# Weight dequantisation one step later, two of its pieces and twelve residual sums beside the feed-forward's first group

## The reference

```python
def nf4_quant_dequant(w):                       # blocks of 64
    absmax = jnp.max(jnp.abs(flat), axis=1, keepdims=True)
    normalized = flat / jnp.where(absmax == 0, 1.0, absmax)
    bounds = (NF4_CODE[:-1] + NF4_CODE[1:]) * 0.5
    idx = jnp.searchsorted(bounds, normalized)
    return (NF4_CODE[idx] * absmax).reshape(shape)
...
q, k, v = h @ Wq, h @ Wk, h @ Wv                # 32 query heads, 8 key-value heads of 128
gs = jax.nn.log_sigmoid(k) / GATE_NORM
o_lin = gla_scan(softmax(q), softmax(k), v, gs) # gated linear attention
y = sliding_window_attn(rope(q), rope(k), v)    # window of 64
o = (0.5 * y + 0.5 * o_lin).astype(bfloat16) @ Wo
...
h = jax.nn.silu(x @ dq1.T) * (x @ dq2.T)        # 512 -> 1376 -> 512
return h @ dq3.T
...
x = x + _layernorm(attention(_layernorm(x)))
x = x + _layernorm(feed_forward(_layernorm(x)))
```

## Time and profile before

| | us |
|---|---|
| median of three runs | 1944.27 |
| the profiled execution | 1944.25 |
| its span, first to last instruction | 1942.5 |
| TensorE busy | 1859.2 (96%) |
| VectorE busy | 1486.0 (77%) |
| ScalarE busy | 1236.8 (64%) |
| GpSimd busy | 1264.9 (65%) |
| mean granted TensorE clock | 0.993 of full speed |
| TensorE waiting for `kt` L945, 29 times | 29.2 |
| TensorE waiting for `xn` at the start, once | 11.5 |
| TensorE waiting for `qtT` L955, 11 times | 9.2 |
| TensorE waiting for `qc` L520, 3 times | 8.6 |

### The profile page before, as it was taken

The page is one execution under the profiler, slowest core; times in us unless marked ns, Lnnn a source line. Parts: engine busy times, 40 slices in busy tenths (PEclk is TensorE's granted clock), DMA queues, the critical chain, the costliest instruction groups (busy, mean ns, idle before and its releaser), DMA issues.

```text
span 1942.5 us, 42961 instructions
## 1 busy us (share of the span) xinstructions
PE 1859.2 (96%) x11566; PEld 1235.4 (64%) x11566; DVE 1486.0 (77%) x3980; ACT 1236.8 (64%) x4840; POOL 1264.9 (65%) x1164
## 2 busy tenths in 40 slices
PE   4899999999999999999999999999999999999997
PEld 3667666766666666766766666766766654444443
DVE  5998888888888888888888888888899956302122
ACT  5677777777777777777777777777667645412121
POOL 2777777777777777777777777777767747212121
PEclk8999999999999999999999999999999999999999
DMA  6111111111111111111111111111201024000000
GB/s 220 55 36 43 41 45 43 43 44 44 43 43 43 42 42 42 43 47 42 42 42 42 42 42 42 42 42 42 84 30 30 23 71 147 33 0 22 0 22 22
DMA packets 85452, 90.52 MB, mean 47 GB/s; under 512 B 14216, under 2 KB 56456, under 8 KB 85384
## 3 DMA queue, kind: packets, MB, share of 16 engines
q1 hardware_dynamic: 85384, 89.71, 14.8%
HBM read 76.48 MB, written 13.18 MB: 46 GB/s over the span
## 4 chain that ended last, share of the span: by engine, by line
PE 62%; DVE 18%; issue 14%; POOL 4%; ACT 1%; DVEq 1%; DMA 0%; POOLq 0%; ACTq 0%
PE bank L1363 17%; PE bank L1352 8%; PE bank L1391 6%; PE bank L1334 4%; PE bank L1407 4%; PE bank L1428 4%; PE bank L1489 4%; PE bank L1400 3%; DVE f_s L1055 2%; PE bank L1318 2%; DVE f_nrm L1042 2%; PE bank L1417 2%; POOL hl L600 2%; PE bank L1507 2%; PE bank L1410 2%
## 5 line engine op out<-in xcount | busy, mean ns | idle before, releaser
L554 POOL TENSOR_TENSOR f_acc<-f_acc,f_s 128x512 f32<-128x512 f32 x429 | 547.5, 1276 | 32.6 <-POOL f_acc L554 0.4
L1363 PE MATMUL bank<-wh,xh 128*128 (+2 forms) x1024 | 334.9, 327 | 6.6 <-DVE cumh L1204 6.0
L1363 PE MATMUL bank<-wl,xh 128*128 (+2 forms) x1024 | 334.8, 327 | 0.0
L1363 PE MATMUL bank<-wh,xl 128*128 (+2 forms) x1024 | 334.6, 327 | 0.0
L538 POOL TENSOR_TENSOR pr<-pr,rp 128x512 f32<-128x512 f32 x128 | 133.2, 1041 | 241.8 <-DVE rp L977 241.5
L1055 DVE TENSOR_SCALAR f_s<-f_nrm 128x512 f32<-128x512 f32 x480 | 260.9, 603 | 3.5
L651 ACT ACTIVATE qe<-bank,nqm 128x128 f32<-128x128 f32 x512 | 180.9, 365 | 108.6 <-DVE qs L906 78.1
L1489 PE MATMUL bank<-xh,w 128*128 (+3 forms) x704 | 218.3, 379 | 1.4 <-ACT sg L832 1.4
L600 POOL TENSOR_TENSOR hl<-hf,hh 128x512 f16<-128x512 f32 (+1 forms) x44 | 51.3, 1167 | 231.9 <-ACT hh L838 231.9
L679 ACT ACTIVATE pr<-bank,pmx 128x128 f32<-128x128 f32 x512 | 180.8, 367 | 32.4 <-DVE pmx L970 24.3
L1214 DVE SCALAR_TENSOR_TENSOR hf<-bank,sg 128x512 f32<-128x512 f32 (+1 forms) x44 | 30.3, 689 | 220.5 <-PE bank L1489 205.9
(11 more groups left out here) (178 smaller groups left out, 4975.0 us busy)
## 6 DMA issues: line engine op xcount, KB each, us to landing
f_blk<-wa SPq DMA_DIRECT2D x33, 320.0 KB, 2.9
f_raw<-wb SPq DMA_DIRECT2D x33, 256.0 KB, 2.7
dequantised<-f_w SPq DMA_DIRECT2D x33, 256.0 KB, 2.0
w<-dequantised SPq DMA_DIRECT2D x33, 256.0 KB, 4.3
raw_qkv<-wq SPq DMA_DIRECT2D x29, 256.0 KB, 2.4
raw_o<-wo SPq DMA_DIRECT2D x29, 256.0 KB, 2.6
f_recb<-scales SPq DMA_DIRECT2D x99, 64.0 KB, 2.6
f_absb<-scales SPq DMA_DIRECT2D x99, 64.0 KB, 2.6
```

The source lines that it names most:

```text
L554: nc.gpsimd.tensor_tensor(f_acc[:], f_acc[:], f_s[:, step, :], ALU.add).then_inc(s["f_ad"], 1)
L1363: last = nc.tensor.matmul(dst, av, w[:, sl + c, lo:hi], start=(n == 0), stop=(n == 3 * NC - 1))
```

## The change

Step 0 makes no comparisons; steps 1 to 31 make pieces 0 to 30, in the turns of the pattern 2, 4, 5, 4. Pieces 31 and 32 are both made beside group 0: 4, 5, 2, 2, 2 comparisons of piece 31 in chunks 1 to 5 and three times 5 of piece 32 in chunks 6 to 8, in the same ring of four slots. The blocks' maxima found in step i are those of piece i, no longer of piece i + 1, and those of piece 32 stand in chunk 2. The low half of a piece (`nf4_low`) goes from the head of turn p = 2 to turn p = 3, after the decays' `gl` and ahead of the comparisons. The twelve residual sums of group 0 go from GpSimd (c = 3 to 5) to VectorE (c = 4 to 6, just ahead of the new rows' statistics). The low halves of a transposed tile are split two ahead and two behind `hidden`. SyncE's tail is put in another order.

```diff
-NF4_STEPS_FIRST = (range(0, 0), range(0, 2), range(2, 8), range(8, 15))
+NF4_FIRST = 1
+NF4_IN_TURNS = STEPS - NF4_FIRST
 NF4_STEPS = (range(0, 2), range(2, 6), range(6, 11), range(11, 15))
...
-        LATE_STEPS = {5: range(0, 3), 6: range(3, 7), 7: range(7, 11), 8: range(11, 15)}
+        LATE_STEPS = {1: (31, range(0, 4)), 2: (31, range(4, 9)), 3: (31, range(9, 11)), 4: (31, range(11, 13)),
+                      5: (31, range(13, 15)), 6: (32, range(0, 5)), 7: (32, range(5, 10)), 8: (32, range(10, 15))}
+        late_number = lambda j, k: 15 * (j - NF4_IN_TURNS) + k
+        late_slot = lambda j, k: late_number(j, k) % 4
...
             with sp.Fori(1, 5) as k:
                 for c in range(NC):
                     load_weights(c, k + 1, k * NC + (NC + c))
-                    nf4_transfers(k * NC + c, 0, 0)
+                    nf4_transfers(k * NC + (c - NF4_FIRST), 0, 0)
...
-            sp.wait_ge(s["f_out"], 16 * 31)
+            sp.wait_ge(s["f_out"], 16 * 30)
...
-            store_piece(31)
-            load_maxima(32, 2)
+            store_piece(30)
+            load_maxima(31, 2)
...
+            store_rows(32)
+            load_piece(32)
+            load_reciprocals(32, 2)
...
-            sp.wait_ge(s["f_ad"], 14 * STEPS)
-            sp.wait_ge(s["f_out"], 16 * STEPS)
-            load_w12(8)
-            load_w12(9)
-            load_w3(9)
             sp.wait_ge(r["x1"], TILES - 2)
             load_w12(10)
+            load_maxima(32, 2)
+            store_piece(31)
+            sp.wait_ge(s["f_out"], 16 * 32)
+            load_w3(9)
             store_piece(32)
             sp.wait_ge(s["f_out"], 16 * NF4_PIECES)
             load_w3(10)
...
-                        if 3 <= c <= 5:
-                            for t in range((c - 2) * STEP, (c - 1) * STEP):
-                                residual(t)
                         if c in LATE_STEPS:
-                            late_add(LATE_STEPS[c])
+                            late_add(*LATE_STEPS[c])
...
+            def residual(t):
+                dve.wait_ge(xr_in[t % (2 * STEP)], 16 * (t // (2 * STEP) + 1))
+                dve.wait_ge(r["z"], t + 1)
+                nc.vector.tensor_tensor(rows[:, t, :], rows[:, t, :], xr[t % (2 * STEP)][:], ALU.add).then_inc(r["x1"], 1)
...
             def turn(t):
-                if t.p == 1 and not (isinstance(t.i, int) and t.i == 0):
-                    nf4_end(t.i - 1)
-                if t.p == 2 and not (isinstance(t.i, int) and t.i == 0):
-                    nf4_low(t.i - 1)
+                if t.p == 1 and not (isinstance(t.i, int) and t.i <= NF4_FIRST):
+                    nf4_end(t.i - (NF4_FIRST + 1))
...
                 log_decay(t)
                 low_decay(t)
-                if t.p > first:
+                if t.p == 3 and not (isinstance(t.i, int) and t.i <= NF4_FIRST):
+                    nf4_low(t.i - (NF4_FIRST + 1))
+                if t.p:
                     nf4(t)
...
-                if t.p == 2 * first:
-                    nf4_blocks(t.i + 1)
-                    nf4_rows(t.i + 1)
+                if t.p == (2 if isinstance(t.i, int) and t.i == 0 else 0):
+                    nf4_blocks(t.i)
+                    nf4_rows(t.i)
...
-            nf4_low(31)
+            nf4_low(30)
             statistics("att", later(1))
+            nf4_scaled(31)
+            late_nf4(*LATE_STEPS[1])
             for c in range(2, FC):
                 if c == TURN_FROM:
                     later_shift("new")
                 if c == FC - 1:
                     nf4_low(32)
-                for item in within[c]:
+                for item in within[c][0:2]:
                     low(item)
                 hidden(0, c)
+                for item in within[c][2:]:
+                    low(item)
                 if c == 2:
-                    nf4_scaled(32)
+                    nf4_blocks(32)
+                    nf4_rows(32)
                     statistics("att", later(2))
                     statistics("att", later(3))
...
                 if 4 <= c <= 6:
+                    for t in later(c - 3):
+                        residual(t)
                     statistics("new", later(c - 3))
+                if c == 6:
+                    nf4_end(31)
+                    nf4_scaled(32)
+                if c == 7:
+                    nf4_low(31)
                 if c in LATE_STEPS:
-                    late_nf4(LATE_STEPS[c])
+                    late_nf4(*LATE_STEPS[c])
```

More of the change, by code:

```diff
@@ L85, in chunk_of @@
     return (j // 2, j % 2) if j < 2 * FC else (j - 2 * FC, 2)
-def nf4_steps(t):
-    return (NF4_STEPS_FIRST if isinstance(t.i, int) and t.i == 0 else NF4_STEPS)[t.p]
 def piece_number(c, kind):
@@ L439, in _ @@
                     load_maxima(0, 0)
+                elif c == 1:
                     store_rows(1)
@@ L444, in _ @@
                 else:
-                    nf4_transfers(c, 0, 0)
+                    nf4_transfers(c - NF4_FIRST, 0, 0)
             with sp.Fori(1, 5) as k:
@@ L483, in _ @@
             load_w3(6)
+            store_rows(32)
+            load_piece(32)
+            load_reciprocals(32, 2)
             load_w12(7)
             load_w3(7)
+            sp.wait_ge(s["f_ad"], 14 * NF4_IN_TURNS)
+            sp.wait_ge(s["f_out"], 16 * NF4_IN_TURNS)
             load_w3(8)
+            load_w12(8)
+            load_w12(9)
             for t in range(2 * STEP, TILES):
                 load_residual(t)
-            sp.wait_ge(s["f_ad"], 14 * STEPS)
-            sp.wait_ge(s["f_out"], 16 * STEPS)
-            load_w12(8)
-            load_w12(9)
-            load_w3(9)
             sp.wait_ge(r["x1"], TILES - 2)
             load_w12(10)
+            load_maxima(32, 2)
+            store_piece(31)
+            sp.wait_ge(s["f_out"], 16 * 32)
+            load_w3(9)
             store_piece(32)
@@ L556, in nf4_add, with late_add @@
             def nf4_add(t):
-                for k in nf4_steps(t):
-                    add_step(t.i, k, 0, k % 8)
-            def late_add(steps):
+                if isinstance(t.i, int) and t.i < NF4_FIRST:
+                    return
+                for k in NF4_STEPS[t.p]:
+                    add_step(t.i - NF4_FIRST, k, 0, k % 8)
+            def late_add(j, steps):
                 for k in steps:
-                    add_step(STEPS, k, 0, k % 4)
+                    add_step(j, k, late_slot(j, 0), late_slot(j, k))
             def residual(t):
@@ L796, in turn @@
                     high(item_at(n))
-                if t.p == 1 and not (isinstance(t.i, int) and t.i == 0):
-                    nf4_high(t.i - 1)
+                if t.p == 1 and not (isinstance(t.i, int) and t.i <= NF4_FIRST):
+                    nf4_high(t.i - (NF4_FIRST + 1))
                 if l1.real():
@@ L864, in _ @@
             high_hidden(0, 1)
-            nf4_high(31)
+            nf4_high(30)
             for c in range(2, FC):
@@ L869, in _ @@
                 silu(0, c)
+                if c == 7:
+                    nf4_high(31)
                 for item in within[c]:
@@ L1045, in nf4 @@
             def nf4(t):
-                j = t.i
-                if t.p == (1 if isinstance(j, int) and j == 0 else 0):
+                if isinstance(t.i, int) and t.i < NF4_FIRST:
+                    return
+                j = t.i - NF4_FIRST
+                if t.p == 0:
                     nf4_scaled(j)
-                for k in nf4_steps(t):
+                for k in NF4_STEPS[t.p]:
                     if k >= 8:
@@ L1056, in nf4, with late_nf4 @@
                                             ALU.is_gt, ALU.mult).then_inc(s["f_sd"], 1)
-            def late_nf4(steps):
+            def late_nf4(j, steps):
                 for k in steps:
-                    if k >= 4:
-                        dve.wait_ge(s["f_ad"], 14 * STEPS + max(k - 4, 1))
-                    nc.vector.tensor_scalar(f_s[:, k % 4, :], f_nrm[:], float(BOUND[k]), float(DELTA[k]),
+                    n = late_number(j, k) - 4
+                    if n >= 0:
+                        dve.wait_ge(s["f_ad"], 14 * (NF4_IN_TURNS + n // 15) + max(n % 15, 1))
+                    nc.vector.tensor_scalar(f_s[:, late_slot(j, k), :], f_nrm[:], float(BOUND[k]), float(DELTA[k]),
                                             ALU.is_gt, ALU.mult).then_inc(s["f_sd"], 1)
@@ L1130, in turn @@
                 l1, l2, l3, n = t.back(1), t.back(2), t.back(3), number(t)
-                first = 1 if isinstance(t.i, int) and t.i == 0 else 0
                 use_k(t)
@@ L1175, in turn @@
                     gla_q(l1)
-                if t.p == first:
+                if t.p == 0:
                     nf4(t)
@@ L1260, in _ @@
             hidden(0, 0)
-            nf4_end(31)
+            nf4_end(30)
             hidden(0, 1)
             add_out(l1)
-            nf4_low(31)
+            nf4_low(30)
             statistics("att", later(1))
+            nf4_scaled(31)
+            late_nf4(*LATE_STEPS[1])
```

7 lines of the change are left out of this document (2 added, 5 removed).

## The result

The changed kernel takes 1954.81 us, the median of five runs (1954.46 to 1955.61), against 1944.27 (1943.83 to 1944.58) before. The ratio is 1.0051, with a 95% interval of 1.0038 to 1.0064: slower by 10.5 us (half a per cent). The forecast was 1956.0. The profiled execution takes 1954.61 with a span of 1952.8, so 10.3 more than that of before.

What follows compares the result with a forecast made beforehand. TensorE was taken as the bound, so a move counts only through its waits. From 1944.25 us, start -7.0, low half +5.2 and +1.2, group 0 +12.7 gave 1956.35, stated as 1956.0, range 1943 to 1969.

Steps and rivals of the forecast that it cites:

- The start: Steps 0 and 1: with piece 0's work gone, TensorE's waits of 7.5 us mostly go; -7.0 us, bounds -8.2 and -5.
- The low half: Fourth turn of loop steps: nf4_low's 0.60 us, less 0.45 regained, costs 0.2 a step (5.2 us); steps 28 to 31 add 1.2.
- rival A: Loop: the low half costs its full 0.60 us a step, giving 1967.6 us; chance 0.17.
- Group 0: Beside group 0: VectorE's added work makes TensorE wait at four places; +12.7 us, ends +5 and +16.
- four places: Group 0, chunks 1 to 3, 4 to 7, 6 and 7, 7 and 8: VectorE's lists delay TensorE by 2.5 + 1.3, 3.2, 3.0, 4.0 us.
- the first place: Chunks 1 to 3: VectorE's added work delays chunk 3's silu 2.5 us; chunk 2's comparisons ahead of `hf` cost 1.3 more.
- the second and third place: Chunks 4 to 7: twelve sums delay chunk 7's silu, 3.2 us; chunks 6 and 7: scaling and comparisons delay `hf`, 3.0.
- B: Group 0 hides the added work, new waits come to about 1.5 us, giving 1945 us; chance 0.17.
- E: Group 0's tail: piece 32's store and load finish late, up to 18 us, giving 1975 us; chance 0.05.
- D: Loop: the low half in the third turn was on the path, so moving it regains 21.3 us, giving 1928.7; chance 0.04.
- The sum: Whole kernel: 1944.25 - 7.0 + 5.2 + 1.2 + 12.7 = 1956.35 us, stated as 1956.0; chance 0.50.

Runs made afterwards that it cites:

- second trace of before: The kernel before run again, unchanged, for a second trace of its start; median 1945.91 us of eight runs, ratio 1.0004.
- filled: Kernel after plus twelve matmuls nobody reads on TensorE ahead of chunk 4 and of chunk 8; 1955.40 us, ratio 1.0051 to before.
- the cut piece: Kernel before with 13 comparisons and 13 sums of piece 0 over 8 columns in place of 512; 1938.18 us, ratio 0.9958.
- start_sums_light: Kernel before with only GpSimd's 13 sums of piece 0 over 8 columns, comparisons kept at 512; 1940.32 us, ratio 0.9969.
- maxima_back: Kernel after with the maxima of piece 0 back in the very first turn; 1955.28 us, ratio 1.0050 to before.

## Why the prediction was right

By its own steps:

- **The start**, -7.0 with bounds -8.2 and -5: measured -9.7, outside them. The waits that go are those named (7.5 to 0.4), and TensorE's idle time falls by 7.8 us where all matmuls are recorded, so as a forecast of the waits the term is sound. The step that failed is the bound, which took the waits for all there is: TensorE's busy time falls by 2.3 too. In the trace of before two stretches at 1.2 GHz stand in the start that after does not have, worth at most 1.0 (0.75 granted at 24 to 28) and 1.7 us (60 to 68). Only the second is behind a wait that the change removes, and the second trace of before has the second and not the first; how much the clock gives the change is thus different from trace to trace.
- **The low half**, 0.2 a step: 0.15 in after, 0.18 alone. The working holds down to its parts: 1.99 in place of 1.81, comparisons shorter, `qe` at 1.04. Steps 2 and 3 cost more (0.45 each), steps 28 on 0.7 for 1.2. The rival A, and with it the full 0.60 that the prediction drew from the lock in the Trainium skill ("SBUF — State Buffer", "Who interferes with whom"), do not come. That the low half itself takes 1.10 beside a sum agrees with the lock.
- **Group 0**, +12.7: measured +14.9. Its four places are there as waits: 2.85 for 2.5, 2.77 for 3.2, 1.94 and 0.55 for 3.0, 4.13 for 3.9. The 1.3 of the earlier trace rows went as said. The waits hide where the 2.2 us too much are; the distances between the products `hf` tell it. From the first to that of chunk 4 it is 36.2 us where it was 31.4: +4.8 for the 3.8 of the first place, and not for the clock, as `filled` shows. From there to chunk 7 it is 32.4 where it was 24.2: +8.1 for the 6.2 of the second and third place. The rest is +2.0 for 2.7. Mis-sized above all were the residual sums. I gave them 0.60 to 0.82; the lines view of VectorE in after has

```profile
L1072 DVE TENSOR_SCALAR f_s<-f_nrm 128x512 f32<-128x512 f32 x30 | 26.6, 947 | 0.1
L1126 DVE TENSOR_TENSOR rows<-rows,xr 128x512 f32<-128x512 f32 x12 | 14.5, 1270 | 0.0
```

  1.27 each (by the issue to the next one 1.2), as slow as on GpSimd (1.32): 14.5 us for the 7.2 of the working. That the term still came near is in part luck, since VectorE's idle time ahead of `hf`, 4.7 us in chunks 4 to 6 of before, took some of them in; the prediction had named that idle time and left it out of its 3.2. The mean hides two cases. The last sum of each four, with GpSimd idle, takes 0.68; of the nine that have GpSimd's additions for a piece or its `hl` beside them eight take 1.16 to 1.76 (and one 0.68):

```profile
1616.19 1.76 DVE L1126 TENSOR_TENSOR rows<-rows,xr 128x512 f32<-128x512 f32 x1
...
1619.44 0.68 DVE L1126 TENSOR_TENSOR rows<-rows,xr 128x512 f32<-128x512 f32 x1
```

  The Trainium skill, "SBUF — State Buffer", section "Who interferes with whom", calls the shared port pair an exclusive lock between VectorE and GpSimd; this case agrees, with 0.68 against 1.76.
- **The rivals.** B fell by what its waits had to be, 12.6 us for 1.5; its first reason was misread besides, since 42.26 in the earlier trace rows is TensorE's weight load, and VectorE was busy 52.42 of the 86 us. E's late tail does not come: TensorE's only wait behind that for `xl` is 0.33, as in before. D falls with the loop, 3.7 us longer.
- **The sum**: the errors are -2.7 at the start, +2.2 in group 0 and -1.1 in the loop and late steps, so that 1956.3 came within 2 us of 1954.6. The mechanism is the one forecast, but the nearness is partly luck: the first two errors nearly cancel, and by the busy time 2.3 of the start's 2.7 are the clock, which the working did not have.

What stays open: how much of group 0's 14.9 is the second stretch at the lower clock (at most 1.7; the fillers remove only the first), and the 3.2 us of the start that the cut piece leaves. The first turn of step 30 took 13.4 us in after and 15.1 in four other traces with the same code there, behind the same wait of 2.5 us for `qtT`; those are granted 0.79 at 1464 to 1472 us where after has 1.00. So any single difference of 2 us may be the clock's.

## What to carry to other kernels

Work that is moved beside a bound engine costs by its place more than by its amount: the same two pieces and twelve sums cost 14.9 us in one order and 6.7 in another (with eight of the sums back on GpSimd), and the order has to be checked against the queue of loads too. Where a wait of TensorE comes or goes, look at the granted clock of the windows behind it, in more than one trace, and then ask whether another engine's list hides it. Match a drop with its wait by the start times: the longest wait of a stretch need not be the one ahead of it. Moving twelve sums of two SBUF operands from GpSimd to VectorE, while GpSimd had other sums to do, brought nothing here (0.4 us the other way).

## What the runs showed of the hardware

- The granted clock fell at the end of single waits of 1.7 to 4.1 us (0.50 to 0.66 in the window of 4 us that holds most of it), but not of each: the wait of 1.7 for `kt` has a drop behind it in both traces of before and none in `start_sums_light`; that of 2.4 for `qc` has one in one trace of before and none in the other; 2.77 us at 1640 to 1643 in after left it at 1.00, and in `maxima_back` it fell there to 0.64 behind 2.70.
- Eight matmuls of chunk 4 are issued about every 0.43 us in place of 0.22 while it is down.
- An addition over 128 x 512 with both operands in SBUF takes 0.68 us on VectorE while GpSimd is idle (three times in after), and 1.16 to 1.76 in eight of nine beside GpSimd's additions; on the mean of four 1.13 to 1.52, about as long as on GpSimd (1.32).
